# Attention probabilities divided by their row sums before the transposes, not after the value product

## The reference

```python
bk, bv = (look_around(bk), look_around(bv))        # keys and values of the block and of the one before
sim = jnp.einsum('bhwid,bhwjd->bhwij', bq, bk)
mask = (i < j) | (i > j + WINDOW) | (j == -1)
sim = jnp.where(mask, -jnp.finfo(sim.dtype).max, sim)
attn = jax.nn.softmax(sim, axis=-1)                # exp(sim - max) / its sum over the keys
out = jnp.einsum('bhwij,bhwjd->bhwid', attn, bv)
...
x = x + o @ wo
```

## Time and profile before

| | |
|---|---|
| runs of the kernel, device us | 969.18 median of 3 (968.12 to 1042.49) |
| the profiled execution, device us | 965.64 |
| its span | 963.9 us, 17473 instructions |
| mean granted clock of TensorE | 0.994 of full |
| PE busy | 914.5 us (95%) |
| DVE busy | 671.2 us (70%) |
| ACT busy | 521.2 us (54%) |
| POOL busy | 405.0 us (42%) |

### The profile page before, as it was taken

The page is one execution under the profiler, slowest core; times in us unless marked ns, Lnnn a source line. Parts: engine busy times, 40 slices in busy tenths (PEclk is TensorE's granted clock), DMA queues, the critical chain, the costliest instruction groups (busy, mean ns, idle before and its releaser), DMA issues.

```text
span 963.9 us, 17473 instructions
## 1 busy us (share of the span) xinstructions
PE 914.5 (95%) x5688; PEld 767.6 (80%) x5688; DVE 671.2 (70%) x1712; ACT 521.2 (54%) x1231; POOL 405.0 (42%) x404
## 2 busy tenths in 40 slices
PE   6999998999999979999998899999999999889998
PEld 4877787878788858888887788887888888778887
DVE  6889998477776687776767456577666677645653
ACT  6785851213131347676666544456667676654443
POOL 2332541022222486767676200017776767621110
PEclk9999999999999989999999999999999999999999
DMA  6202013000000000000000210000000000000001
GB/s 246 77 17 66 23 45 114 1 1 0 0 1 1 23 1 1 25 0 23 0 11 29 82 36 10 4 27 2 1 24 0 23 0 25 19 14 17 30 26 48
DMA packets 15732, 26.34 MB, mean 27 GB/s; under 512 B 1658, under 2 KB 12272, under 8 KB 14912
## 3 DMA queue, kind: packets, MB, share of 16 engines
q1 hardware_dynamic: 15680, 25.69, 8.2%
HBM read 20.53 MB, written 2.10 MB: 23 GB/s over the span
## 4 chain that ended last, share of the span: by engine, by line
PE 74%; DVE 15%; ACT 4%; issue 2%; POOL 2%; SPq 2%; DMA 1%; DVEq 0%; ACTq 0%; POOLq 0%
PE bank L1662 33%; PE bank L2042 5%; PE bank L1996 5%; PE bank L2006 5%; PE bank L1897 5%; PE bank L2020 5%; PE bank L1983 2%; DVE scanned L765 2%; DVE normed L1184 2%; PE bank L1841 2%; PE bank L1975 2%; PE bank L1860 1%; SPq L371 1%; PE bank L2030 1%; DVE y L855 1%
## 5 line engine op out<-in xcount | busy, mean ns | idle before, releaser
L1530 ACT ACTIVATE probs<-bank,row_min 128x256 f32<-128x256 f32 (+1 forms) x256 | 110.4, 457 | 99.6 <-DVE row_min L1108 99.6
L1108 DVE CUSTOM_DVE_ANT_0 bank<-bank,mask 128x256 f32<-128x256 f32 (+1 forms) x256 | 90.6, 425 | 5.9 <-PE bank L1996 5.7
L581 POOL TENSOR_TENSOR norms<-norms,minus_half 128x16 f32<-128x16 f32 x32 | 93.6, 2924 | 2.7
L1662 PE MATMUL bank<-wqkv_hi,x_hi 128*128 128x512 f32 x192 | 82.4, 429 | 1.8 <-DVE rot L1083 1.1
L1662 PE MATMUL bank<-wqkv_lo,x_hi 128*128 128x512 f32 x192 | 76.6, 399 | 0.0
L1662 PE MATMUL bank<-wqkv_hi,x_lo 128*128 128x512 f32 x192 | 75.7, 394 | 0.0
L1246 DVE SCALAR_TENSOR_TENSOR hidden<-bank,lcols,hidden 128x512 f32<-128x512 f32 (+1 forms) x48 | 36.0, 749 | 51.9 <-PE bank L1662 28.2
L1129 DVE TENSOR_TENSOR inner<-inner,bank 128x256 f32 (+1 forms) x32 | 13.5, 421 | 80.0 <-PE bank L2042 80.0
L563 POOL TENSOR_TENSOR q_tok<-rot 128x512 f32<-128x512 f32 x32 | 41.0, 1281 | 58.6 <-DVE rot L1083 58.6
L2006 PE MATMUL bank<-ident,probs 128*128 128x128 f32 x448 | 61.4, 278 | 2.4 <-ACT probs L1530 2.4
L1662 PE MATMUL bank<-t_hi,wm_hi 128*128 128x512 f32 x160 | 63.6, 397 | 0.0
(11 more groups left out here) (266 smaller groups left out, 2599.0 us busy)
## 6 DMA issues: line engine op xcount, KB each, us to landing
w_stage<-in_wm_l_dram SPq DMA_DIRECT2D x8, 534.0 KB, 3.6
w_stage<-in_wqkv_dram SPq DMA_DIRECT2D x2, 1536.0 KB, 7.6
out_dram<-stream SPq DMA_DIRECT2D x8, 256.0 KB, 2.5
inner<-in_w_gate_dram SPq DMA_DIRECT2D x1, 1152.0 KB, 10.0
stream<-in_x_dram SPq DMA_DIRECT2D x2, 512.0 KB, 5.6
stream<-in_x_dram SPq DMA_DIRECT2D x1, 1024.0 KB, 12.5
ew<-in_pos_bias_dram SPq DMA_DIRECT2D x1, 1024.0 KB, 14.5
inner<-in_w_x_dram SPq DMA_DIRECT2D x1, 1024.0 KB, 6.9
```

What stands on the lines that cost most here:

```text
L581: pool.tensor_tensor(norms[:, 2, :], norms[:, 1, :], minus_half[:, :], ALU.pow).then_inc(c_rn, 1)
L1108: dve.tensor_tensor_reduce(logits, logits, mask[:, 2 * P - nk:2 * P], 1.0, FAR, ALU.add, ALU.min, row_min[:, w % 2, 2 * i + e:2 * i + e + ...
L1530: act.activation(probs[:, i, e, 0:nk], logits, ACT.Exp, bias=row_min[:, w % 2, h:h + 1], scale=-1.0, accum_out=row_sum[:, w % 2, h:h + 1]) ...
L1662: ins = pe.matmul(out, stationary, moving, start=(first and i == 0), stop=(last and i == len(terms) - 1))
```

## The change

The division by the row sums moves ahead of the transposes. A new step of DVE, `shares`, runs twice a window, once for each half of the heads: it waits for that half's four exponentials, inverts their four sums, waits for its own result, and multiplies four heads of `probs` (128 x 1024 elements, or 128 x 512 where w = 0) in place by the inverses. The probability transposes of PE wait for `c_share` of their half, where they waited for the exponentials. `invert_sums`, `spread_sums`, `transpose_sums`, `sums_transposed` and `normalise` go, with their tiles; the copy of bank 3 to `o_t` goes to ACT (`weighed`), between the squares of q and the keys. The first `shares` stands where `normalise` stood, ahead of `norm_keys`; the second stands where `invert_sums` stood, ahead of the rotary products.

```diff
--- before.py
+++ after.py
@@ -211,8 +211,6 @@
         h_t = sb("h_t", [P, KD, T])
         shifts = (shifted, squares[:, 0, :].rearrange("p (t c) -> p t c", c=P))
         st_att = ExitStack()
-        rsum_heads = sb("rsum_heads", [P, HEADS, DH], stack=st_att)
-        rsum_t = sb("rsum_t", [P, INNER], stack=st_att)
         o_t = sb("o_t", [P, KI, P], stack=st_att)
         k_t = sb("k_t", [P, KI, T], stack=st_att)
         probs = sb("probs", [P, KI, 2, 2 * P], stack=st_att)
...
@@ -563,13 +561,6 @@
                     pool.tensor_tensor(dst[:, par, :], rot[:, 2 * i, :], rot[:, 2 * i + 1, :], ALU.add)\
                         .then_inc(c_add, 1)
 
-            def spread_sums(n):
-
-                pool.wait_ge(c_rt, n)
-                wait_alone(pool, c_ri, n + 1)
-                pool.tensor_copy(rsum_heads[:, :, :], row_rsum[:, :].unsqueeze(2).to_broadcast([P, HEADS, DH]))\
-                    .then_inc(c_rb, 1)
-
             def rnorm(n, par):
 
                 pool.wait_ge(c_ss, n + 1)
@@ -613,7 +604,6 @@
             def window(n, t, w, l, b, two, three):
                 if three:
                     copy_tile(n + 3, t + 3, (w + 3) % 2, l * NB + b + 1 if w == 0 else l * NB + b + 2)
-                spread_sums(n)
                 if two:
                     rotate(n + 2, w % 2)
                 elif w == 2:
@@ -1108,20 +1098,16 @@
                     dve.tensor_tensor_reduce(logits, logits, mask[:, 2 * P - nk:2 * P], 1.0, FAR, ALU.add, ALU.min,
                                              row_min[:, w % 2, 2 * i + e:2 * i + e + 1]).then_inc(c_tt, 1)
 
-            def invert_sums(n, w):
-
-                dve.wait_ge(c_ex, 8 * n + 8)
-                dve.wait_ge(c_rb, n)
-                dve.reciprocal(row_rsum[:, :], row_sum[:, w % 2, :]).then_inc(c_ri, 1)
-
-            def normalise(n):
-
-                dve.wait_ge(c_rt_out, n + 1)
-                dve.wait_ge(c_pv, n + 1)
-                if not (isinstance(n, int) and n == 0):
-                    dve.wait_ge(c_wo, n)
-                dve.tensor_tensor(o_t[:, :, :].rearrange("p c t -> p (c t)"), bank[3][:, :], rsum_t[:, :], ALU.mult)\
-                    .then_inc(c_ot_out, 1)
+            def shares(n, w, half):
+
+                nk = 2 * P if w else P
+                heads = slice(4 * half, 4 * half + 4)
+                dve.wait_ge(c_ex, 8 * n + 4 * half + 4)
+                dve.reciprocal(row_rsum[:, heads], row_sum[:, w % 2, heads]).then_inc(c_ri, 1)
+                dve.wait_ge(c_ri, 2 * n + half + 1)
+                p = probs[:, :, :, :].rearrange("p i e k -> p (i e) k")[:, heads, 0:nk]
+                dve.tensor_tensor(p, p, row_rsum[:, heads].unsqueeze(2).to_broadcast([P, 4, nk]), ALU.mult)\
+                    .then_inc(c_share, 1)
 
             def att_residual(n, tile):
 
@@ -1132,11 +1118,10 @@
                 for half in range(2):
                     for e in range(2):
                         masked(n, w, half, e)
-                if prev:
-                    normalise(n - 1)
+                shares(n, w, 0)
                 if one:
                     norm_keys(n + 1, (w + 1) % 2)
-                invert_sums(n, w)
+                shares(n, w, 1)
                 if two:
                     rope_products(n + 2, (w + 2) % TT, 0)
                     rope_products(n + 2, (w + 2) % TT, 1)
@@ -1305,7 +1290,6 @@
                         window(n0 + b * TT + w, b * TT + w, w % TT, l, True, True, True, True)
                 for w in range(1, TT):
                     window(n0 + NT - TT + w, NT - TT + w, w, l, True, w < 3, w < 2, False)
-                normalise(n0 + NT - 1)
                 att_residual(n0 + NT - 1, NT - 1)
                 dve.wait_ge(d_zero, l + 1)
                 for b in range(NB):
@@ -1543,11 +1527,13 @@
                 else:
                     act.activation(probs_ts[i][:, 0:4:2, :], src[:, 0:4:2, :], ACT.Copy).then_inc(c_pt_out, 1)
 
-            def sums_transposed(n):
-
-                act.wait_ge(c_rt, n + 1)
-                act.wait_ge(c_ot_out, n)
-                act.activation(rsum_t[:, :], bank[3][:, :], ACT.Copy).then_inc(c_rt_out, 1)
+            def weighed(n):
+
+                act.wait_ge(c_pv, n + 1)
+                if not (isinstance(n, int) and n == 0):
+                    act.wait_ge(c_wo, n)
+                act.activation(o_t[:, :, :].rearrange("p c t -> p (c t)"), bank[3][:, :], ACT.Copy)\
+                    .then_inc(c_ot_out, 1)
 
             def window(n, w, l, prev, one, two, three):
                 for half in range(2):
@@ -1555,6 +1541,8 @@
                         exps(n, w, half, e)
                 if two:
                     square(n + 2, 0)
+                if prev:
+                    weighed(n - 1)
                 if one:
                     keys(n + 1, (w + 1) % TT)
                 if two:
@@ -1566,7 +1554,6 @@
                 if one:
                     queries(n + 1)
                 probs_transposed(n, w, KI - 1)
-                sums_transposed(n)
                 if two:
                     values(n + 2, (w + 2) % TT)
                 if three:
@@ -1650,6 +1637,7 @@
                         window(n0 + b * TT + w, w % TT, l, True, True, True, True)
                 for w in range(1, TT):
                     window(n0 + NT - TT + w, w, l, True, w < 3, w < 2, False)
+                weighed(n0 + NT - 1)
                 with act.Fori(0, NB - 1) as b:
                     mlp(l * NB + b, l, True)
                 mlp(l * NB + NB - 1, l, False)
@@ -2000,7 +1988,7 @@
 
             def transpose_probs(n, w, i):
 
-                pe.wait_ge(c_ex, 8 * n + 4 * (i // 2) + 4)
+                pe.wait_ge(c_share, 2 * n + i // 2 + 1)
                 for e in range(2):
                     for k in range(2 if w else 1):
                         ins = pe.transpose(bank[SCORES[i // 2] + i % 2][:, (2 * e + k) * P:(2 * e + k + 1) * P],
@@ -2011,7 +1999,8 @@
 
                 pe.wait_ge(c_pt_out, 4 * n + 4)
                 pe.wait_ge(c_v, n + 1)
-                pe.wait_ge(c_rt_out, n + 1)
+                if not (isinstance(n, int) and n == 0):
+                    pe.wait_ge(c_ot_out, n)
                 nk = 2 if w else 1
                 for i in range(KI):
                     for k in range(nk):
@@ -2021,15 +2010,6 @@
                                             v_tok[:, w - nk + 1 + k, h * DH:(h + 1) * DH],
                                             probs_ts[i][:, 2 * e + k, :], start=(k == 0), stop=(k == nk - 1))
                 ins.then_inc(c_pv, 1)
-
-            def transpose_sums(n):
-
-                pe.wait_ge(c_rb, n + 1)
-                pe.wait_ge(c_ot_out, n)
-                for i in range(KI):
-                    ins = pe.transpose(bank[3][:, i * P:(i + 1) * P],
-                                       rsum_heads[:, 2 * i:2 * i + 2, :].rearrange("p e d -> p (e d)"), ident[:, :])
-                ins.then_inc(c_rt, 1)
 
             def project_o(n, keyed):
 
@@ -2060,7 +2040,6 @@
                 if one:
                     transpose_q(n + 1, (w + 1) % 2)
                 transpose_probs(n, w, KI - 1)
-                transpose_sums(n)
                 if two:
                     qkv(n + 2, (w + 2) % TT, 2)
                 if three:
```

More of the change, by code:

```diff
@@ L249, in build @@
         (c_zero, c_tab, c_xs, c_xt, c_xt_out, c_p, c_sq, c_v, c_ss, c_clip, c_rn, c_rq, c_rope, c_add,
-         c_kn, c_t, c_kt, c_qt, c_qk, c_tt, c_ex, c_pt, c_pt_out, c_pv, c_ri, c_rb, c_rt, c_rt_out, c_ot_out,
+         c_kn, c_t, c_kt, c_qt, c_qk, c_tt, c_ex, c_pt, c_pt_out, c_pv, c_ri, c_share, c_ot_out,
          c_wo, c_res) = signals(
             "c_zero c_tab c_xs c_xt c_xt_out c_p c_sq c_v c_ss c_clip c_rn c_rq c_rope c_add c_kn c_t "
-            "c_kt c_qt c_qk c_tt c_ex c_pt c_pt_out c_pv c_ri c_rb c_rt c_rt_out c_ot_out c_wo c_res")
+            "c_kt c_qt c_qk c_tt c_ex c_pt c_pt_out c_pv c_ri c_share c_ot_out c_wo c_res")
         (d_shift, d_stats, d_aggr, d_eps, d_rstd, d_norm, d_tp, d_tp_out, d_w1, d_gelu, d_act, d_w2, d_res0) = signals(
```

## The result

The changed kernel took 974.53 us (median of 5 runs, 973.54 to 975.77), the kernel before 968.70 (median of 5). The ratio is 1.0076 with a 95% interval of 1.0061 to 1.0090: 7.4 us slower (5.9 to 8.7), clear of noise, under 2%. One of the five runs before took 1042.49 us and is left out of the ratio. The two medians are 5.8 us apart, which is just under the lower end of that interval. The forecast was 9.3 us slower, at 978.5 us.

A forecast was written before the change was run, and what follows sets the result against it. The prediction took PE as the bound, with the change's DVE work and its meetings with POOL lengthening windows; terms summed to +9.3 us on 969.2, giving 978.5 us, 8-in-10 range 965 to 990 us.

The forecast's parts named there:

- PE's loss: Four transposes of the sums leave PE in each window: 0.35 us, 11.2 us over 32 windows if PE stayed the bound.
- ACT and POOL: ACT's moved 0.60 us copy fits its 0.83 us wait for the keys; POOL loses an unawaited copy: both free.
- The multiplication: DVE's product of probabilities and inverses, twice a window: 1.22 us for 128x1024, 0.68 us where w = 0.
- POOL in the way: In w = 2 and 3, POOL's `wm_lo` subtraction stretches DVE's first multiplication by 0.6 us: period +0.3 us, 12 windows.
- the upper case: In w = 2 and 3, POOL's copy gets between first multiplication and `norm_keys`: period up to 0.5 us longer.
- w = 1: PE waits 0.7 us for the scaled keys, then for the second multiplication: +0.45 us, 8 windows.
- w = 0: Shorter multiplications leave PE alone, but POOL's work falls on both: -0.2 us, between -0.35 and +0.5, 6 windows.
- The ends: First windows +0.3 us each, n = 14 +0.2 each plus +1.5 once for the clock, last windows +0.4 each.
- the clock drop: Behind the key transposes of n = 14, PE's longer wait brings half clock in both layers: +1.5 us once.
- PE as the bound: Rival: every multiplication hides behind PE and only 11.2 us less remains: 958 us; 8%.
- POOL getting in a second time: Rival: POOL gets in again behind `norm_keys`; w = 2 or 3 grow by 0.9 us: 996 us; 15%.
- stretch of half clock: Rival: PE's waits drop the clock inside 26 windows, 1.5 us each: 1008 us or more; 4%.

The follow-up runs named there:

- The control: The kernel before, with POOL's split of the feed-forward weights moved behind the spread of the sums, ahead of its rotary sums: 967.20 us, ratio 1.0005.
- the moved split: The changed kernel, with POOL splitting the feed-forward weights behind the second multiplication, ahead of its rotary sums: 963.87 us, ratio 0.9975 to the kernel before.
- keys first: The changed kernel with DVE's scaling of the keys ahead of the first multiplication: 967.87 us, ratio 1.0008 to the kernel before.
- the keys on POOL: The changed kernel with POOL's weight split behind the second multiplication and the keys scaled by POOL instead of DVE: 961.99 us, ratio 0.9951.
- the second subtraction: The changed kernel with POOL's weight subtraction done twice, one behind the other, at its old place: 985.05 us, ratio 1.0185 to the kernel before.

## Why the prediction held

- **PE's loss** was mis-sized: 0.35 us a window by the gap behind the sums' transposes, 0.44 us by the kernel without multiplications. The gap ahead of them (0.44 us from the last probabilities at 444.77, which the earlier trace rows leaves out, to 445.21) was the right one; the product behind starts early and its first matmul takes the 0.09 us back (0.48 against 0.39 us). Over the 26 windows of the middle that is 2.3 us, the largest error of a term, and a part of why w = 0 and w = 1 came out lower.
- **ACT and POOL** free: shown, but for the 0.1 us with w = 1, by the kernel without multiplications.
- **The multiplication** at 1.22 us: 1.23 where POOL idles.
- **POOL in the way**: the step as put. Forecast was a stretch of 0.6 us of the first multiplication and a period 0.2 to 0.5 us longer, taken as 0.3; measured are 0.66, 0.20 more on the keys, and +0.23. The link that waits is another one than worked out: the prediction had PE waiting for the rotary products of q; it waits for the keys. The keys were worked out for 442.31, 0.28 us ahead of PE, and the 0.6 us of stretch were then put on the rotary products but not on the keys. With it they are late by the prediction's own numbers. In the trace the rotary products of q end 0.1 us ahead of the v third, so the two chains give nearly the same period. The copy that gets in between the multiplication and the keys was the upper case (0.5); it happened, and cost 0.2.
- **w = 1**: +0.45 forecast, +0.24 in the windows of the loop. DVE's chain was right (the keys are what PE waits for, 0.50 us there too); the period was too long by PE's 0.09 us and by a second wait, 0.15 us for the second multiplication, which the trace doesn't have.
- **w = 0**: between the bounds, better than taken: -0.35, all but 0.1 us of what the window could give (11.32 us without multiplications, 11.41 with).
- **The ends**: too low by 2.6 us. n = 0 of layer 1 has PE waiting 6.4 us, with 6.8 us at half clock around it, against 4.2 and 3.4 before. Not all of that is the change: before, another 3.4 us at half clock lie just ahead, from 344.8 us, which the changed kernel doesn't have there, and PE waits 5.7 us without multiplications too. The control (split moved in the kernel before) comes to its first residual 1.7 us later than the kernel before, at the same time for the whole. So how much of the 1.0 us that n = 0 of layer 1 adds belongs to the change is open. In n = 14 the clock drop came in both layers, as put. In n = 15 the prediction left out that PE would wait 2.1 us for the first multiplication, and that the clock could drop there too; of its 2.2 us in layer 1, 1.25 are gone in layer 2, where the clock drop is missing.
- **Rivals.** PE as the bound is refuted for this kernel, and is what the moved split reaches in w = 2 and 3. POOL getting in a second time exists (its copy, ahead of the keys), but costs 0.2 us; a window with w = 2 or 3 grew by 0.23 us, not 0.9. No stretch of half clock stands in the middle of either layer.

That the sum of 9.3 us came within 2 us of the measured 7.4 and within 1 of the profile's 8.3 is in part luck, since errors of both signs met: the middle was too dear by 3.7 us, the ends too cheap by 2.6.

The rule of the Trainium skill ("SBUF — State Buffer", section "SBUF: two separate sides"), an exclusive lock for the whole instruction between a DVE instruction with two SBUF inputs and a GpSimd instruction that reads SBUF, agrees in kind with the traces here, in both directions: DVE waits for POOL's subtraction (1.89 us), POOL's copy waits for DVE (1.39 us), and which one blocks is decided by 0.06 us of start time (keys first). But the loss stays about 0.15 us under the overlap: of the 0.96 us of subtraction, 0.81 lay over the multiplication and cost 0.66; with the keys on POOL 0.86 us cost 0.71.

## What to carry to other kernels

When work moves onto an engine with slack, put it into that engine's timeline at its place and list what the neighbour that shares its port does there, after the change and not before: here the move of POOL's queue by 1 us made a meeting that the old trace doesn't show. It cost 8 us in the 12 windows with w = 2 and 3, as much as the whole change lost. If such a meeting is found, the other engine's work can be moved into its idle time: here that cost one wait and gave back more than the change had lost. And a table of waits names the link that is late, not the cause. The waits for the keys in the middle of a layer came from the length of the multiplication in front of them: with the keys first they were gone, and the window with w = 1, where nothing meets, was as long as before to 0.05 us.

## What the runs showed of the hardware that was not expected

- Between two DVE instructions that follow each other with no gap, a POOL instruction that is waiting gets in: the copy behind the first multiplication (the keys 0.88 us), the second subtraction (the keys 1.43 us). DVE did not keep POOL out in either.
- A wait of PE of 2.53 us was followed by half clock in one layer and not in the other of the same execution; over the runs the stretches at the ends of the layers come and go, at 0.9 to 1.5 us each in n = 14 (with the moved split it takes 12.44 us at full clock in layer 1 and 13.81 us with a stretch in layer 2; with the keys first 12.31 us without and 13.17 with one). Kernels that differ by 2 us there can't be ranked by one profile.
